# Second edge attention of a four-layer graph network: running maxima by scans over the sorted edges in place of per-node tables

## The reference, cut to what matters

```python
xh = (x @ W).reshape(N, H, D)
a_src = jnp.einsum('nhd,hd->nh', xh, att_src)
a_dst = jnp.einsum('nhd,hd->nh', xh, att_dst)
e = jax.nn.leaky_relu(a_src[src] + a_dst[dst], NEG_SLOPE)      # the edges and one loop for each node
m = jax.ops.segment_max(e, dst, num_segments=N)
e = jnp.exp(e - m[dst])
denom = jax.ops.segment_sum(e, dst, num_segments=N)
alpha = e / denom[dst]
out = jax.ops.segment_sum(xh[src] * alpha[:, :, None], dst, num_segments=N).reshape(N, H * D) + bias
```

## Time and profile before

| what | us |
|---|---|
| median of 3 runs (lowest, highest) | 8025.69 (8011.5, 8032.68) |
| the profiled execution, time | 8034.18 |
| the profiled execution, span | 8031.9 |
| first attention, edge loop | from about 600 to 2170 |
| second attention | from 6511 to 7854 |
| final stage | from 7854 to 8032 |

### The profile page before, as it was taken

The page is one execution under the profiler, slowest core; times in us unless marked ns, Lnnn a source line. Parts: engine busy times, 40 slices in busy tenths (PEclk is TensorE's granted clock), DMA queues, the critical chain, the costliest instruction groups (busy, mean ns, idle before and its releaser), DMA issues. The chain is left out here.

```text
span 8031.9 us, 101344 instructions
## 1 busy us (share of the span) xinstructions
PE 6812.9 (85%) x30971; PEld 3926.6 (49%) x30971; DVE 5413.0 (67%) x12509; ACT 1518.2 (19%) x4812; POOL 4516.3 (56%) x4616
## 2 busy tenths in 40 slices
PE   1379999999859999899999999989999868888883
PEld 1136666666535444455555544444444444444442
DVE  8788999999876666644444444444444488888887
ACT  0021111111110000000000045500000044444441
POOL 1005555555457777777777711167777636666660
PEclk9999999999979999999999999999999999999997
DMA  0256666666643333354444544433333444444443
GB/s 8 56 204 174 173 172 171 173 172 173 165 133 101 96 98 98 99 118 135 131 130 132 135 146 162 162 114 104 103 105 103 103 142 115 114 114 113 114 110 99
DMA packets 462335, 1016.96 MB, mean 127 GB/s; under 512 B 114227, under 2 KB 229471, under 8 KB 455158
## 3 DMA queue, kind: packets, MB, share of 16 engines
q0 software_dynamic: 240960, 702.53, 32.7%
q1 hardware_dynamic: 220854, 308.06, 11.9%
HBM read 849.27 MB, written 160.73 MB: 126 GB/s over the span
## 5 line engine op out<-in xcount | busy, mean ns | idle before, releaser
L764 PE MATMUL psum<-rows,oh 128*128 128x257 f32 (+2 forms) x8800 | 2708.4, 406 | 362.8 <-DMA rows<-h_tab,src_i 119.0
L862 PE MATMUL psum<-ident,ones 128*128 128x512 bf16 x9419 | 2516.8, 381 | 0.0
L771 DVE TENSOR_TENSOR acc<-acc,psum 128x264 f32 (+2 forms) x3520 | 1480.6, 421 | 1143.3 <-PE psum L764 1065.0
L764 PEld LDWEIGHTS psum<-rows,oh 128*128 128x128 f32 x8800 | 1497.5, 190 | 1322.2 <-issue 421.0
L729 POOL DMA_INDIRECT rows<-qv_tab,src_i x880 | 872.3, 991 | 1241.4 <-SPq L2706 560.0
L862 PEld LDWEIGHTS psum<-ident,ones 128*128 128x128 bf16 x9419 | 912.4, 99 | 820.3 <-issue 14.3
L729 POOL DMA_INDIRECT rows<-xh_tab,src_i x880 | 835.0, 949 | 613.4 <-PE psum L764 312.9
L729 POOL DMA_INDIRECT rows<-h_tab,src_i x880 | 912.6, 1037 | 291.2 <-issue 242.5
L729 POOL DMA_INDIRECT rows<-h_tab,wts x880 | 875.3, 995 | 268.1 <-issue 241.0
L729 POOL DMA_INDIRECT rows<-hw_tab,rel_i x880 | 857.3, 974 | 283.8 <-issue 222.1
L771 DVE TENSOR_TENSOR kh<-kh,psum 128x257 f32 x880 | 371.6, 422 | 634.8 <-PE psum L764 631.5
(11 more groups left out here) (393 smaller groups left out, 7314.1 us busy)
## 6 DMA issues: line engine op xcount, KB each, us to landing
wts<-hots SPq DMA_DIRECT2D x220, 256.0 KB
hw_tab<-acc SPq DMA_DIRECT2D x50, 1024.0 KB, 4.1
part_tab<-rows SPq DMA_DIRECT2D x50, 512.0 KB
rows<-part_tab SPq DMA_DIRECT2D x50, 512.0 KB, 5.3
hots<-oh SPq DMA_DIRECT2D x74, 256.0 KB, 2.7
rows<-qv_tab,src_i POOLq DMA_INDIRECT x880, 3.7
rows<-h_tab,src_i POOLq DMA_INDIRECT x880, 2.8
rows<-h_tab,wts POOLq DMA_INDIRECT x880, 2.8
```

The costliest lines, as they stand in the source:

```text
L764: nc.tensor.matmul(psum[:, banks[b % len(banks)], 0:width], oh[:, b // GROUP, b % GROUP], rows[:, b, at:at + width], start=True, stop=True ...
L771: nc.vector.tensor_tensor(to, to, psum[:, banks[b % len(banks)], 0:width], ALU.add).then_inc(acc_done, 1)
L862: nc.tensor.matmul(bank, ones[:, :].bitcast(BF16)[:, 0:P], busy, start=True, stop=True)
```

## The change

`sum_attention` is replaced by `edge_attention`, with the first attention's way of finding maxima.

- The score of an edge is now made by PE (`edge_scores`): one f32 product with the identity brings the source scores out of the eight gathered rows, and three bf16 products for each slot (24 for a group, each of eight columns) add the destination's score in three parts, straight out of the table `adst` at a place that is read from memory, plus a constant offset. DVE forms the leaky ReLU (`lean_scores`, two operations).
- Then `turn_scores`, `scan_within`, `row_of_ends`, `join_slots`, `spread_bounds`, `scan_across` as in the first attention.
- `differences` gives score minus maximum on PE, and ACT takes the exponential out of PSUM. `top_of_edges` turns the maxima back, and DVE writes those of a node's last edge as columns 264 to 271 of the gathered rows (`keep_top`). The sums, and `acc`, become 272 columns wide, so the node's maximum is summed along, and the tables `mnode`, `new_tile` and `flags` go, and with them `take_best`, `update_maxima`, `shift_scores` and `fetch_halves`.
- The rows are held 272 numbers wide in 24 places in place of 16 rows of 520.
- `keep_warm` matmuls: eight for each group in place of 16.
- The stage that lays out the edges loses the DMA of `flags` and eight DMAs from it into `starts` (L442), and gains a comparison, two matmuls of one partition's row and an addition (`last` now marks only a node's last edge over all slots). SP loads the marks of the breaks group by group in the second attention too, two DMAs of 16 KB for each group.
- The 50-tile clearing of `acc` comes behind the release of the other engines. The final stage forms the maxima in two more operations on 128x400.

```diff
@@ edge_attention, PE
+        def edge_scores(pe, g, places):
+            for n in range(g * GROUP, (g + 1) * GROUP):
+                pe.wait_ge(*row_in(n))
+            pe.wait_ge(score_ready, done(g - 1))
+            nc.tensor.matmul(ps_edge, ident[:, :], value_heads(g)[:, :, :, DH], start=True, stop=False)
+            pe.wait_ge(oht_sb, done(g))
+            for s in range(GROUP):
+                node = adst.bitcast(U8)[:, bass.ds(places[s], 4 * ADSTW)].bitcast(BF16)[:, 1::2]
+                for k in range(3):
+                    mm = nc.tensor.matmul(ps_edge[:, s * HEADS:(s + 1) * HEADS], oht16[g % 2][:, s],
+                                          node[:, k * HEADS:(k + 1) * HEADS], start=False, stop=(s, k) == (GROUP - 1, 2))
+            mm.then_inc(edge_ps, 1)
+        def top_of_edges(pe, g):
+            pe.wait_ge(alpha_ready, done(g))
+            nc.tensor.matmul(ps_top, across[g % 2][0:GH], ident[0:GH, 0:GH], start=True, stop=True).then_inc(top_ps, 1)
+            for g in groups:
+                sums_of(pe, g, range(0, 4))
+                if more:
+                    edge_scores(pe, g + 1, places)
+                sums_of(pe, g, range(4, 5))
+                if more:
+                    turn_scores(pe, g + 1)
+                sums_of(pe, g, range(5, 6))
+                if more:
+                    row_of_ends(pe, g + 1)
+                if later:
+                    turn_hot(pe, g + 2)
+                sums_of(pe, g, range(6, 7))
+                if more:
+                    keep_busy(2)
+                    spread_bounds(pe, g + 1)
+                    fall_of_node(pe, g + 1)
+                sums_of(pe, g, range(7, 8))
+                if more:
+                    keep_busy(1)
+                    differences(pe, g + 1)
+                    top_of_edges(pe, g + 1)
+                    keep_busy(5)
@@ edge_attention, DVE
+        def lean_scores(dve, c, g):
+            dve.wait_ge(edge_ps, g + 1)
+            c.then(v.tensor_scalar(mine, edge, 0.2, None, ALU.mult))
+            v.tensor_tensor(mine, mine, edge, ALU.max).then_inc(score_ready, 1)
+        def keep_top(dve, c, g):
+            dve.wait_ge(top_ps, g + 1)
+            ends = last[:, g * GROUP:(g + 1) * GROUP].unsqueeze(2).to_broadcast([P, GROUP, HEADS])
+            c.step(nc.vector.tensor_tensor(group_rows(g)[:, :, ACCW:SUMW], ps_top.rearrange("p (h s) -> p s h", s=GROUP),
+                                           ends, ALU.mult))
+            for g in groups:
+                places = acc_places(g * GROUP, GROUP)
+                lower_sums(dve, c, g, places[0])
+                weigh_values(dve, g, 0)
+                weigh_values(dve, g, 1)
+                c.wait()
+                add(dve, g, 0, places)
+                weigh_values(dve, g, 2)
+                add(dve, g, 1, places)
+                if more:
+                    lean_scores(dve, c, g + 1)
+                weigh_values(dve, g, 3)
+                add(dve, g, 2, places)
+                if more:
+                    scan_within(dve, g + 1)
+                add(dve, g, 3, places)
+                if more:
+                    join_slots(dve, c, g + 1)
+                add(dve, g, 4, places)
+                if more:
+                    scan_across(dve, c, g + 1)
+                add(dve, g, 5, places)
+                if more:
+                    keep_top(dve, c, g + 1)
+                add(dve, g, 6, places)
+                add(dve, g, 7, places)
@@ the stage that lays out the edges
-        for h in range(HEADS):
-            sp.dma_start(starts[h * GROUP:(h + 1) * GROUP, :, :],
-                         flags.rearrange("(g s) e -> s g e", s=GROUP)).then_inc(starts_in, 16)
-        sp.wait_ge(starts_in, 16 * HEADS)
```

More of the change, by code:

```diff
@@ L33 @@
 KHW = D + 1
+SUMW = ACCW + HEADS
 ROW = 2 * D + HEADS
@@ L500, in reload_tensor @@
             mm = nc.tensor.matmul(psum[0:1, b, 0:SLOTS // 2], ident[:, P - 1:P], ends_f[:, half], start=True, stop=True)
+        mm.then_inc(marks_turned, 1)
+        pe.wait_ge(marks_ready, 3)
+        for b in range(2):
+            half = slice(b * SLOTS // 2, (b + 1) * SLOTS // 2)
+            mm = nc.tensor.matmul(psum[:, 2 + b, 0:SLOTS // 2], last_node, last_slot[:, half], start=True, stop=True)
         mm.then_inc(marks_turned, 1)
@@ new lines, in turn_scores, with row_of_ends @@
+        def turn_scores(pe, g):
+            pe.wait_ge(score_ready, done(g))
+            pe.wait_ge(weight_ready, done(g - 1))
+            nc.tensor.matmul(ps_score, padded[g % 2][:, 0:2 * GH], flipped, start=True, stop=False)
+            nc.tensor.matmul(ps_score, padded[g % 2][:, GH:], ident[:, :], start=False, stop=True).then_inc(score_ps, 1)
+        def row_of_ends(pe, g):
+            pe.wait_ge(within_ready, nth(g))
+            nc.tensor.matmul(ps_row, within[g % 2][:, P - 1:P], paired, start=True, stop=True).then_inc(row_ps, 1)
@@ new lines, in spread_bounds, with fall_of_node @@
+        def spread_bounds(pe, g):
+            pe.wait_ge(bound_ready, nth(g))
+            for k in range(2):
+                mm = nc.tensor.matmul(ps_bound[:, k:k + 1], bound[g % 2][:, k::2], ones[0:1, 0:1], start=True, stop=True)
+            mm.then_inc(bound_ps, 1)
+        def fall_of_node(pe, g):
+            pe.wait_ge(wide_ready, nth(g))
+            pe.wait_ge(oht_sb, done(min(g + 1, groups[-1])))
+            node = oh[0:1, g % 2, 0]
+            nc.tensor.matmul(ps_fall, node, by_link(bound[g % 2])[:, :, 0], start=True, stop=False)
+            nc.tensor.matmul(ps_fall, node, inherited[g % 2], start=False, stop=True).then_inc(alpha_ps, 1)
@@ new lines, in differences, with sums_of @@
+        def differences(pe, g):
+            pe.wait_ge(across_ready, nth(g))
+            nc.tensor.matmul(ps_diff, ident[:, :], score[g % 2], start=True, stop=False)
+            nc.tensor.matmul(ps_diff, across[g % 2][0:GH], negated[0:GH], start=False, stop=True).then_inc(diff_ps, 1)
+        def top_of_edges(pe, g):
+            pe.wait_ge(alpha_ready, done(g))
+            nc.tensor.matmul(ps_top, across[g % 2][0:GH], ident[0:GH, 0:GH], start=True, stop=True).then_inc(top_ps, 1)
+        def sums_of(pe, g, slots):
+            pe.wait_ge(wide_ready, nth(g))
@@ new lines, in sums_of, with keep_busy, on_tensor @@
+                pe.wait_ge(acc_done, summed(n - len(banks)))
+                nc.tensor.matmul(psum[:, banks[n % 4], 0:SUMW], oh[:, g % 2, s], held(n),
+                                 start=True, stop=True).then_inc(agg_done, 1)
+        def keep_busy(count):
+            keep_warm(psum[:, 2, :], count)
+        def on_tensor(pe):
+            pe.wait_ge(begun, 2)
+            places = places_of(0)
+            turn_hot(pe, 0)
+            edge_scores(pe, 0, places)
+            turn_hot(pe, 1)
+            turn_scores(pe, 0)
+            row_of_ends(pe, 0)
+            spread_bounds(pe, 0)
+            fall_of_node(pe, 0)
+            differences(pe, 0)
+            top_of_edges(pe, 0)
+            for g in groups:
+                more, later = g + 1 in groups, g + 2 in groups
```

570 lines of the change are left out of this document (231 added, 339 removed).

## The result

The changed kernel takes **8224.2 us** (8220.87 to 8233.22), the kernel before 8023.14 beside it: a ratio of **1.0247**, interval 1.0235 to 1.026. The forecast was 8058, with a range of 7970 to 8135. Slower was the right side, but the loss is 200 us and not 35.

A forecast was written before the change was run, and what follows sets the result against it. The second attention was taken as bound by a cycle through several engines, 12.03 us a group, becoming 12.4: 110 x 0.37 = +41 us, other parts -9, so 8034.2 + 41 - 9 = 8066, median 8058 us, range 7970 to 8135.

The forecast's parts named there:

- Step 3: Second attention, PE's edge_scores behind the fourth sum: identity product 0.2 us, then 24 small products with register addresses 1.5 us.
- the lower end: Least price for the 24 small products in edge_scores: 0.049 us each, 1.2 us at least, against 3.1 at most.
- The first rival: Register operations pace PE's 24 small products at 0.128 us each: cycle 13.06 (8130 us) or 13.96 (8229 us); chance 0.2.
- 4 to 7: Second attention: leaky ReLU 0.49 us, scores to scan_across 4.45, differences to keep_top 1.10 + 0.15, additions and lowering 1.51.
- The 0.1 that I added for hand-overs: Allowance per group for hand-overs and uneven groups, raising the 12.31 us walk of the second attention to 12.4.
- the third rival: PE's clock falls to 1.2 GHz in the second attention with half the filler gone: over 3 us a group, +330; chance 0.03.
- ahead of `keep_top`: Sign of being right: in the second attention DVE waits 0.5 to 1 us for PE before keep_top.
- Ahead of `lean_scores`: Sign of being right: in the second attention DVE waits 1 to 2 us for PE before lean_scores' first operation.
- The layout stage: Without the eight loads of starts DVE sets the stage's end, near 334.5: -11 us, between -8 and -13.
- The other parts: Changes outside the second attention's cycle: layout stage -11 us, final stage and the stage ahead of it +2, together -9.
- The 81 ns a pair of the Trainium skill: Alternative price for edge_scores' small products, weight load and matmul together: 1.94 us instead of 1.5, result 8106; not adopted.
- The faster rival: DVE's waits in the second attention fall under other work, cycle drops towards the gathers' 10.0 us: 7794 or 7959; chance 0.17.

The follow-up runs named there:

- the moved kernels: Changed kernel with the edge_scores products moved a group earlier, behind top_of_edges; without five fillers ahead 8198.7 us (1.0225) and 1.02, with them 1.0201 to 1.0225.
- the fixed addresses: Changed kernel with the 24 small products reading node scores at addresses fixed when written (wrong nodes' scores): 8013.4 us (0.999); at the lower clock 9350.5 us (1.0264).
- before_one_load: Kernel before with one of eight loads of starts kept in the layout stage, the rest zeroed on POOL: 8916.8 us, ratio 0.9979, at the lower clock.
- changed_again: The changed kernel itself measured once more, against the kernel before: 8218.1 us, ratio 1.0235.
- no_filler_in_place: Changed kernel with the products in their place and only the five fillers behind top_of_edges removed: 9131.2 us, ratio 1.0232, at the lower clock.
- walk_early: Changed kernel with one 24-column product a slot, moved behind the previous group's last sum, three fillers ahead, leaky ReLU and small products earlier: 7988.4 us, ratio 0.9958.

## Why the prediction was wrong, step by step

Measured in the group shown above, against the walk of the forecast:

| step | forecast | measured | from |
|---|---|---|---|
| 1 first weighing to first sum | 0.80 | 0.79 | 7011.42 to 7012.21 |
| 2 four sums | 1.91 | 1.90 | to 7014.11 |
| 3, with the hand-over of 4: identity, 24 products, to DVE | 0.2 + 1.5 + 0.2 | 2.93 | to 7017.04 |
| 4 leaky ReLU | 0.49 | 0.57 | to 7017.61 |
| 5 scores to end of scan_across | 4.45 | 4.57 | to 7022.18 |
| 6 to keep_top, and keep_top | 1.25 | 1.31 | to 7023.49 |
| 7 additions and lowering | 1.51 | 1.62 | to 7025.11 |
| sum | 12.31 | 13.69 | |

- **Step 3 is the one that failed.** The forecast has 1.5 us for the 24 products, 0.063 each, and they took 2.63. 1.03 of the 1.38 us lie here, 112 us over 109 groups. The reason given, "PE's queue can begin some of this under the four sums, so I take 1.5, near the lower end", was half right. The queue does begin there, 1.1 us ahead, and hides 0.83 us. But the price below it was wrong: a product whose address has a register in it costs 0.144 once the head start is used up, three times the 0.049 of the lower end, and fifteen of the 24 pay it.
- **The first rival** had the mechanism, with a chance of 0.2, and hid 0.9 us, near the measured 0.83. Its two prices, 13.06 and 13.96, enclose 13.69, but its price for one product was too low: ACT's 0.128 is 1.02 / 8, which counts the whole length of the last copy (0.23). From start to start ACT's copies lie (1.02 - 0.23) / 7 = 0.113 apart. That the average of PE's 24, 0.110, lies so near is luck: it mixes nine products at 25 ns with fifteen at 144.
- **The mean over the small steps.** 4 to 7 together came out 0.37 longer than forecast (40 us): lean_scores 0.08, the walk to the scans 0.12, steps 6 and 7 0.17. Each is within the estimate's grain, but all have one sign. The 0.1 that I added for hand-overs was too little.
- **The clock and the mean.** The mean cycle is 13.88, the undisturbed one 13.69: 0.19 us, 21 us in all. 27 of the 109 distances hold a stretch under full clock, with a mean of 14.50; the other 82 have a median of 13.68. But the kernel of before has five such, with a mean of 13.95, and its 12.03 is a mean as well, with a median of 11.87. The forecast set a walk made of undisturbed rows against that mean, which alone makes it 0.16 us too low. What the third rival took from the change is the difference, (27 x 0.82 - 5 x 2.08) / 109 = 0.11 us, and not the +330 us of its price. The half-clock stretches cost far more in the moved kernels.
- **What held.** The walk is what bounds, and DVE's saved work turned into waits: ahead of `keep_top` 0.84 (0.5 to 1 expected). Ahead of `lean_scores` it is 2.65, over the expected 1 to 2, by step 3. POOL waits 463.7 / 94 = 4.9 us a group for sums, and no wait for rows is left. The layout stage ends at 334.54 (near 334.5). The other parts are -12.2 + 1.5 = -10.7 (-9).
- **The 81 ns a pair of the Trainium skill** (TensorE: Matmul & The Clock Gate, section Back-to-back issue gap) stands there for matmuls of 128 columns. By it, an estimate, step 3 would have been 1.94 us and the result 8106. It was nearer in the sum, but by luck: no pair here takes 81 ns, they take 25 with a fixed address or under the head start and 144 with a register behind it.
- **The faster rival** needed DVE's waits to fall under other work. The written order doesn't let them: with the products at 0.62 us the cycle is still 11.93, and only with the walk moved as well do groups of 10.60 appear. Even the fixed addresses bring no more than the old time (0.999).

## What to carry to other kernels

Price instructions whose addresses have registers in them in two parts. As many as the queue has prepared come at the plain pace, here nine, the others at the pace of the register operations, here 0.144 us. Read a pace from start to start, not as total time by count. A row from another engine (ACT's 0.113) gives the kind of cost and not its size. One instruction with three times the columns was cheaper than three. When small products are moved, ask whether they fit into the new place, with the register loads behind them, and look at the granted clock there: a dense stretch made thin can give back at half clock what the shorter path gains. And sum the walk with rows of the same shape, then add for each hand-over, since small errors there have one sign.

## What the runs showed that I had not expected

- A small bf16 product with its 128x128 weight load started every 25 ns at a fixed address, and at one of a register and an offset every 144 ns on the average once the queue's head start was used up. The register operation itself takes 105 ns for the first of a slot's three products and 46 for the other two. Behind it, the next load begins about 50 ns later, the product 7 ns behind the load and the next register operation 22 ns behind that: 124 and 183 ns, the two distances found. Why the slot's first is longer stays open:

```profile
L1280 PEldq FUSED_REGOPS  x2640: 46/46/128, 6512.1 to 8029.8; - x189
```

- The whole program ran at times at a lower granted clock (0.92 over the span for before_one_load, a kernel otherwise like the one of before, whose clock was 0.976), and 11 to 14% longer. It isn't a matter of the chip alone: changed_again and no_filler_in_place ran on the same one, with 8028 and 8925 us for the kernel of before. In the changed kernel there, DVE gets the products' result 1.8 us after their records end (L1280 from 8007.60 for 2.76 us, L1436 at 8012.16), and TensorE shows nothing in between but the next sum, which ends at 8011.02:

```profile
8010.32 0.70 PE L1325 MATMUL psum<-rows,oh 128*128 128x272 f32 x2
...
8012.16 0.27 DVE L1436 TENSOR_SCALAR wts<-psum 128x64 f32<-128x64 f32 x1 [4.49 <-remote]
...
8012.80 0.49 PE L1287 MATMUL psum<-wts 128*128 128x128 f32 x2 [1.78 <-DVE wts L1437]
```

The ends of matmuls are modelled, so the records can't say what TensorE did in those 1.8 us. Neither this nor the cause of the lower clock was settled.
- A kernel's rank can turn with that clock: the fixed addresses stood at 0.999 of the kernel before and at 1.0264, walk_early at 0.9958 and, with three fillers more, at 0.974 to 0.976.
